# Building weighted one-hot tiles in float32 from a ring of twelve, with four PSUM banks, and moving the direct products to the node update's bank

## The reference

```
h = relu(layernorm(x))
m = relu(concat(h[src], edge_attr) @ W1 + b1) @ W2 + b2
x = x + relu(concat(h, segment_sum(m, dst)) @ U1 + c1) @ U2 + c2
h = relu(layernorm(x))
x = x + segment_sum(h[src] * edge_weight[:, None], dst)
```

## Time and profile before

| what | value |
|---|---|
| median of three runs | 2679.72 us (2676.95 to 2680.86) |
| profiled execution, its time | 2659.47 us |
| its span, first to last instruction | 2657.7 us |
| busy PE, DVE, ACT, POOL | 2049.9, 1311.2, 974.0, 1691.7 us |
| gathers issued | from 63.2 to 2203.6 us |
| first piece loaded in the second stage | 2219.6 us |
| granted TensorE clock, mean | 0.888 |

### The profile page before, as it was taken

The page is one execution under the profiler, slowest core; times in us unless marked ns, Lnnn a source line. Parts: engine busy times, 40 slices in busy tenths (PEclk is TensorE's granted clock), DMA queues, the critical chain, the costliest instruction groups (busy, mean ns, idle before and its releaser), DMA issues.

```text
span 2657.7 us, 57208 instructions
## 1 busy us (share of the span) xinstructions
PE 2049.9 (77%) x21651; PEld 1747.1 (66%) x21651; DVE 1311.2 (49%) x4334; ACT 974.0 (37%) x2419; POOL 1691.7 (64%) x1659
## 2 busy tenths in 40 slices
PE   5766666777777877777787777877778878999998
PEld 5555555656665666666666666766666767787886
DVE  6655555555555555556555555555555551111122
ACT  3334344444444444444444444444444441000111
POOL 6777777777777777777777777777777771000000
PEclk9988888888888888888888898889899899999998
DMA  3455444454444444334333333333223226999995
GB/s 88 129 169 173 162 159 159 165 171 140 142 140 148 130 132 135 118 119 127 106 109 113 99 97 94 87 94 85 74 74 82 65 62 240 401 377 384 372 350 163
DMA packets 422423, 414.27 MB, mean 156 GB/s; under 512 B 288562, under 2 KB 374178, under 8 KB 416000
## 3 DMA queue, kind: packets, MB, share of 16 engines
q1 hardware_dynamic: 369348, 354.89, 38.6%
q0 software_dynamic: 52064, 53.17, 8.8%
q10 hardware_dynamic: 732, 2.48, 0.4%
HBM read 258.64 MB, written 151.74 MB: 154 GB/s over the span
## 4 chain that ended last, share of the span: by engine, by line
POOL 62%; issue 19%; PE 9%; DMA 8%; DVE 1%; DVEq 0%; SPq 0%; ACT 0%; POOLq 0%
POOL rows L608 62%; DMA stage<-adjacency 7%; PE pair L1032 5%; PE pair L1039 1%; PE pair L1022 1%; PE pair L1045 1%; PE pair L864 1%; DMA x_all<-in_x_dram 1%; PE pair L852 0%; DVEq L1363 0%; PE pair L960 0%; PE pair L1053 0%; DVE nodes L1368 0%; DVE mean L1140 0%; SPq L490 0%
## 5 line engine op out<-in xcount | busy, mean ns | idle before, releaser
L608 POOL DMA_INDIRECT rows<-table,idx x1616 | 1649.4, 1021 | 512.0 <-issue 492.2
L721 ACT COPY stage<-pair 128x300 f32<-128x300 f32 x1616 | 622.3, 413 | 689.8 <-PE pair L946 687.3
L946 PE MATMUL pair<-bld 128*128 128x300 bf16 x4848 | 813.1, 316 | 4.5 <-DVE bld L1329 4.5
L923 PE MATMUL pair<-w1b,rings 128*128 128x128 f32 x1616 | 307.1, 349 | 530.4 <-DVE rings L1305 530.3
L923 PEld LDWEIGHTS pair<-w1b,rings 128*128 128x128 f32 x1616 | 261.2, 246 | 588.3 <-DVE rings L1305 587.9
L946 PEld LDWEIGHTS pair<-bld 128*128 128x128 bf16 x4848 | 552.2, 120 | 134.7 <-DVE bld L1329 7.9
L1329 DVE TENSOR_TENSOR bld<-bld,part 128x512 bf16<-128x512 bf16 x1212 | 432.4, 410 | 0.0
L1323 DVE TENSOR_TENSOR bld<-iota_lo,lo 128x512 bf16<-128x512 f16 x404 | 172.5, 427 | 471.1 <-PE pair L946 468.3
L1325 DVE TENSOR_SCALAR bld<-iota_key,key 128x300 bf16<-128x300 f16 x1616 | 383.5, 300 | 0.0
L1305 DVE TENSOR_TENSOR rings<-rows,pair 128x512 f32<-128x512 f32 x202 | 138.3, 685 | 461.4 <-DMA rows<-table,idx 461.4
L1032 PE MATMUL pair<-stage,h 125*64 125x96 f32 x5870 | 297.4, 253 | 25.0 <-DMA stage<-adjacency 22.2
(11 more groups left out here) (131 smaller groups left out, 779.3 us busy)
## 6 DMA issues: line engine op xcount, KB each, us to landing
stage<-adjacency SPq DMA_DIRECT2D x270, 480.0 KB, 9.4
rings<-in_edge_attr_dram SPq DMA_DIRECT2D x202, 256.0 KB
adjacency<-stage SPq DMA_DIRECT2D x28, 1200.0 KB
rows<-table,idx POOLq DMA_INDIRECT x1616
adjacency<-stage SPq DMA_DIRECT2D x20, 1080.0 KB
adjacency<-stage SPq DMA_DIRECT2D x20, 960.0 KB
adjacency<-stage SPq DMA_DIRECT2D x20, 840.0 KB
adjacency<-stage SPq DMA_DIRECT2D x20, 720.0 KB
```

The lines of the kernel that those rows point to most:

```text
L608: pool.indirect_dma_start(out=rows[:, slot, t, :], out_offset=None, in_=table, in_offset=bass.IndirectOffsetOnAxis(ap=idx[:, g, t:t + 1], ...
L721: act.copy(tiles[:, g % STAGE, :, t * WT:(t + 1) * WT], build_bank[i % 3][:, 0:KEYS].rearrange("p (h w) -> p h w", w=WT)).then_inc(tile_ke ...
L923: last = pe.matmul(bank[:, a * P:(a + 1) * P], eaT[:, slot, a, :], w1b2[:, :], start=True, stop=True)
L946: last = pe.matmul(build_bank[i % 3][:, 0:KEYS], hot_w[q % 2][k][:, :, u], hot_key[q % 2][:, u, :], start=(k == 0), stop=(k == PARTS - 1))
```

## The change

The quads go. make_tile makes the operands of one tile in float32 with two instructions: a comparison of a row of 128 numbers with `lo`, multiplied by the weight in the same instruction, and a comparison of 300 numbers with `key`. The operands lie in a ring of twelve tiles (HOTS) and VectorE is eight tiles ahead (AHEAD). build_tile issues one float32 matmul into one of four banks, instead of three bfloat16 ones into three. `key`, `lo` and the weight are kept in float32; the split of the weight ahead of the loop is gone, and so is one constant that GpSimd made. The fourth bank was `u_bank[0]` of the direct products; these now use 96 columns at the end of the second half of pair 1, whose first 375 are the node update's. Since a bank is shared, the two take turns: the node update begins at an odd step (UPDATE[c] = SUMMED[c] | 1: 23, 43, 63, 83, 103, 123, 143, 165, 185, 203), its three parts are two steps apart, and each waits until the direct product before it was copied out, as the direct products wait for the update's copies. READY[c] is UPDATE[c] + 8. The loops have three more steps at the end.

```diff
-    READY = [SUMMED[c] + 6 for c in range(CHUNKS)]
+    UPDATE = [SUMMED[c] | 1 for c in range(CHUNKS)]
+    READY = [UPDATE[c] + 8 for c in range(CHUNKS)]
...
-        build_bank = [pair[2][:, 0, :], pair[2][:, 1, :], pair[3][:, 0, :]]
+        mid_bank = pair[1][:, 1, 0:SPLIT * NP]
+        direct_bank = pair[1][:, 1, 512 - COLS:512]
+        build_bank = [pair[2][:, 0, :], pair[2][:, 1, :], pair[3][:, 0, :], pair[3][:, 1, :]]
...
             def build_tile(g, t):
                 i = g * T + t
-                q, u = i // 4, i % 4
-                if u == 0:
-                    pe.wait_ge(quad_made, q + 1)
-                wait_count(pe, tile_kept, i - 2)
-                for k in range(PARTS):
-                    last = pe.matmul(build_bank[i % 3][:, 0:KEYS], hot_w[q % 2][k][:, :, u], hot_key[q % 2][:, u, :],
-                                     start=(k == 0), stop=(k == PARTS - 1))
-                last.then_inc(tile_built, 1)
+                pe.wait_ge(tile_hot, i + 1)
+                wait_count(pe, tile_kept, i - BUILDS + 1)
+                pe.matmul(build_bank[i % BUILDS][:, 0:KEYS], hot_w[:, i % HOTS, :], hot_key[:, i % HOTS, :], start=True,
+                          stop=True).then_inc(tile_built, 1)
...
             def direct(b, half):
...
+                for c in range(CHUNKS):
+                    since = 2 * b + 2 + half - UPDATE[c]
+                    if since in (1, 3):
+                        pe.wait_ge(g_staged, 2 * c + (since + 1) // 2)
+                    if since == 5:
+                        pe.wait_ge(x1_made, c + 1)
...
             def make_g(c, half):
+                wait_count(pe, direct_kept, direct_by(UPDATE[c] + 2 * half))
...
-            dve.tensor_copy(part[0][:, :, :], wgt).then_inc(w_split, 1)
-            dve.tensor_tensor(w_left, wgt, part[0][:, :, :], ALU.subtract).then_inc(w_split, 1)
...
-            def make_quad(q):
-                g, t = q // 2, q % 2 * 4
-                wait_count(dve, tile_built, 4 * (q - 1))
-                dve.tensor_tensor(hot_eq[q % 2], iota_lo[:, :, :], over(lo[:, g, t:t + 4], P), ALU.is_equal).then_inc(eq_made, 1)
-                for u in range(4):
-                    dve.tensor_scalar(hot_key[q % 2][:, u, :], iota_key[:, :], key[:, g, t + u:t + u + 1], None,
-                                      ALU.is_equal)
-                dve.wait_ge(eq_made, q + 1)
-                for k in range(PARTS):
-                    last = dve.tensor_tensor(hot_w[q % 2][k], hot_eq[q % 2], over(part[k][:, g, t:t + 4], P), ALU.mult)
-                last.then_inc(quad_made, 1)
+            def make_tile(i):
+                g, t = i // T, i % T
+                wait_count(dve, tile_built, i - HOTS + 1)
+                dve.tensor_scalar(hot_w[:, i % HOTS, :], iota_key[:, 0:P], lo[:, g, t:t + 1], wgt[:, g, t:t + 1],
+                                  ALU.is_equal, ALU.mult)
+                dve.tensor_scalar(hot_key[:, i % HOTS, :], iota_key[:, :], key[:, g, t:t + 1], None,
+                                  ALU.is_equal).then_inc(tile_hot, 1)
```

More of the change, by code:

```diff
@@ L9 @@
 I32 = mybir.dt.int32
-BF16 = mybir.dt.bfloat16
-F16 = mybir.dt.float16
 AX_X = mybir.AxisListType.X
@@ L31 @@
 STAGE = 4
+HOTS = 12
+AHEAD = 8
 SPLIT = 3
@@ L219, in build @@
         rel = sb("rel", [P, GROUPS, T])
-        key = sb("key", [P, GROUPS, T], F16)
-        lo = sb("lo", [P, GROUPS, T], F16)
-        part = [sb(f"part{k}", [P, GROUPS, T], BF16) for k in range(PARTS)]
+        key = sb("key", [P, GROUPS, T])
+        lo = sb("lo", [P, GROUPS, T])
+        wgt = sb("wgt", [P, GROUPS, T])
         rings = sb("rings", [P, 3 * TWO * T * D + TWO * T * (D + 1)])
@@ L233, in build @@
         key_now = sb("key_now", [P, T])
[L236 to L250, removed]
+        bld = sb("bld", [P, HOTS * (P + KEYS)])
+        assert PIECES * 4 * BLK * GC <= STAGE * ROW
+        hot_w = bld[:, 0:HOTS * P].rearrange("p (s e) -> p s e", s=HOTS)
+        hot_key = bld[:, HOTS * P:].rearrange("p (s c) -> p s c", s=HOTS)
         s_back = bld[:, 0:SLOTS * COLS].rearrange("p (s c) -> p s c", s=SLOTS)
@@ L747, in fast_groups @@
                 keep_eaT(1, 1, ea_bank)
-                for s in range(GROUPS + 6):
+                for s in range(GROUPS + 9):
                     if s < GROUPS:
@@ L978, in make_up @@
                 pe.wait_ge(g_staged, 2 * c + 2)
+                wait_count(pe, direct_kept, direct_by(UPDATE[c] + 4))
                 for b in range(BLK):
@@ L1340, in fast_groups @@
             def fast_groups():
-                make_quad(0)
-                make_quad(1)
-                for s in range(GROUPS + 6):
+                for i in range(AHEAD):
+                    make_tile(i)
+                for s in range(GROUPS + 9):
                     if s < GROUPS:
@@ L1348, in fast_groups @@
                         add_sums(s - 1)
-                    for q in (2 * s + 2, 2 * s + 3):
-                        if q < 2 * GROUPS:
-                            make_quad(q)
+                    for i in range(s * T + AHEAD, (s + 1) * T + AHEAD):
+                        if i < TILES:
+                            make_tile(i)
                     for c in range(CHUNKS):
-                        if s == SUMMED[c] + 3:
+                        if s == UPDATE[c] + 5:
                             add_up(c, mid_bank[0:NP, 0:BC])
                             centre(2)(c, 0)
-                        if s == SUMMED[c] + 4:
+                        if s == UPDATE[c] + 6:
                             variance(2)(c, 0)
-                        if s == SUMMED[c] + 5:
+                        if s == UPDATE[c] + 7:
                             stage_h2(c, 0)
```

52 lines of the change are left out of this document (20 added, 32 removed).

## The result

The changed kernel takes 2786.12 us (median of 4 runs, 2776.16 to 2802.28), the kernel before, run beside it, 2680.29: a ratio of 1.0403, 95% interval 1.0352 to 1.0454. It is 4% slower; 2595 us, 3% faster, was forecast. The profiled execution took 2776.16 us.

A forecast was written before the change was run, and what follows sets the result against it. GpSimd's gathers, by number times length plus issue, were taken to bound the first stage. Terms -113.6 + 19 + 3 + 6.5 = -85 us gave 2679.7 - 85 = 2595 us, range 2566 to 2655.

The forecast's parts named there:

- The bound: First stage: time is the number of gathers times their length plus 0.305 us issue each; no gather waits for `pre_made`.
- What is removed: Gathers: lengthening beside the old VectorE instructions and weight split goes, -113.6 us; about 10.3 of 123.9 us remain.
- the gather waits for the streaming part alone and gets in between two instructions of a row: Gathers beside new VectorE instructions: held only 159 or 68 ns per instruction, as read off L1325.
- +19 us: Gathers' first need, 0.13 us in: waits for the new instructions' streaming part, 66 ns mean when held; bounds 0 and 80.
- the +3 us at the end: Gathers' end: 0.09 us can be made up, only the 159 ns instruction exceeds that; bounds 0 and 19 us.
- Rival (2): Gathers beside VectorE rows: rows without a pause shut them out until the row is over; +104 us, 2699 us; chance 0.12.
- the count of 29: Gathers that started within 50 ns ahead of three L1329 and waited for the third's end; taken as 29 of 202 rows.
- The rule that I weighed: Gathers: a VectorE instruction locks GpSimd out for its whole length; 80 instead of 19 us, 2656 us; chance 0.10.
- PE: Matmuls: 300-column records 0.25 us apart, a group costs 0.9 us more, hidden under the gathers.
- The second stage: After the gathers: later READY makes 11 pairs of batch and chunk be stored and loaded again, +6.5 us (5.6 to 7.0).
- New lengths: VectorE's new float32 comparisons: 378 ns for 300 numbers and 287 ns for 128.
- The range of the forecast: Whole kernel: 2566 to 2655 us; the forecast's own case, 2580 to 2615 us, had chance 0.60.

The follow-up runs named there:

- turns alone: The kernel before with UPDATE, READY, the waits and the direct products' bank of the changed kernel, quads and bfloat16 kept: ratio 0.9996.
- changed, another session: The changed kernel unaltered, run again beside its version with three build banks: ratio 1.0119 to the kernel before.
- three banks: The changed kernel with three build banks instead of four, nothing else: ratio 0.996 to the kernel before.
- three banks, another session: The changed kernel with three build banks instead of four, run again beside the four-bank one: ratio 1.0152 to the kernel before.
- ring of six: The changed kernel with HOTS 6 and AHEAD 4 instead of 12 and 8, four banks kept: 2654.36 us in one execution.
- pause at every tile: The changed kernel, but VectorE waits for the end of a tile's pair of comparisons before starting the next pair: 2602.69 us in one execution.
- pause at every second: The changed kernel, but VectorE waits for its own end at every second tile, making rows of four instructions: 2588.63 us in one execution.
- wide one in PSUM: The changed kernel with three build banks; only the comparison of 300 numbers reads its row from PSUM: 2580.84 us in one execution.
- weighed one in PSUM: The changed kernel with three build banks; only the weighed comparison of 128 numbers reads its row from PSUM: 2554.2 us in one execution.
- both in PSUM: The changed kernel with three build banks; both comparisons of a tile read their row of numbers from PSUM: 2549.0 us, ratio 0.9528.
- the four-bank kernel of the same session: The changed kernel unaltered, run again in a session in which engines stand still: ratio 1.0227 to the kernel before.

## Why the prediction was wrong

**The bound** was read rightly: 62 to 64% of the chain is POOL's, no gather waits. The sum over the median accounts for all that followed. Span less that sum, in the ordinary sessions (us):

| kernel | span | over the median | rest |
|---|---|---|---|
| before | 2657.7 | 123.9 | 2533.8 |
| turns alone | 2668.3 | 132.0 | 2536.3 |
| changed | 2774.3 | 239.4 | 2534.9 |
| changed, another session | 2726.2 | 189.8 | 2536.4 |
| three banks | 2653.5 | 116.6 | 2536.9 |
| three banks, another session | 2732.7 | 194.8 | 2537.9 |
| ring of six | 2652.5 | 109.0 | 2543.5 |
| pause at every tile | 2600.9 | 62.9 | 2538.0 |
| pause at every second | 2586.8 | 48.5 | 2538.3 |
| wide one in PSUM | 2579.0 | 43.0 | 2536.0 |
| weighed one in PSUM | 2552.4 | 14.0 | 2538.4 |
| both in PSUM | 2547.2 | 9.1 | 2538.1 |

The rest stays within 10 us in all of them, through 218 us more busy time of TensorE's tile matmuls (1031.4 against 813.1), other rings, banks and turns.

**What is removed** was right in kind and size: of 123.9 us some 10 were to stay, and with new instructions that read PSUM 9.1 do.

**The step that failed** is "the gather waits for the streaming part alone and gets in between two instructions of a row. I take that over". It was read off rows of four 16-bit instructions and carried to rows of sixteen float32 ones. The new rows leave less room: in the changed kernel no gather that was held for over 0.10 us got in behind an L1308, and those that got in behind an L1310 had often missed the same place before (once in the gather of 2049.39 us, five times in that of 1991.64). The count that it was read off is short too: of some 300 gathers that are 0.13 us in while an L1325 runs 68 are lengthened, 38 by an L1325 and the rest by the L1323 or L1329 that had not ended yet. In place of +19 us the new instructions cost 239.4 - 9.1 = 230 us in one profile and 181 in the other. It covers both terms, the +19 us at the start (131 measured) and the +3 us at the end (106), which rested on a VectorE instruction that could be held off for 0.09 us; the gathers were held off instead. Rival (2), at 0.12, came nearest: rows shut gathers out for more than 3 us. But it had them all wait to the row's end, which 36 of the 122 long ones do, took over the count of 29 where 124 are over 0.56 us longer, and did not have the shut-outs at the end at all; its 104 us stand against some 180 to 230. The step is shown false by the pause, which brings back most of the loss with every instruction unchanged. With rows out of the way the single instructions cost 34 and 5 us, 39 together beside the forecast's 19 for both, and not in its order: most of it was to be the wide one's.

The rule that I weighed, that the lock lasts for the whole instruction (the Trainium skill's page "SBUF — State Buffer", section "SBUF: two separate sides"), gave 80 us. The traces agree with its distance at the end of a gather (0.13 us measured, about 0.115 stated) and with its warning, but not with the size: a lock for the length of one instruction alone makes no wait of 3.2 us beside instructions of 0.37, as at 1991.64 us. The page says nothing of rows.

**PE** was right: the changed kernel's two records of a tile are 0.253 us apart in the median at full clock, and PE still waits for the sums that VectorE makes of the gathered rows, and not the gathers for PE:

```profile
DVE rings L1290 <- DMA rows<-table,idx: 1065.2, 200, 9.5
...
PE pair L913 <- DVE rings L1290: 474.3, 162, 7.1
```

**The second stage** was to grow by 6.5 us. To be read beside the earlier trace rows:

```profile
2334.80 1.40 SPq L482 DMA_DIRECT2D stage<-adjacency  x3
```

```profile
2334.80:2774.30 439.50, 401.56 (x6620) 344.62 (x6620) 71.49 (x321) 47.62 (x207) 0.00 (x0) 0.98 0.96 350
```

The stage takes 439.5 us against 438.1; 441.8 and 442.4 with the turns alone and with both comparisons in PSUM. So it grew by 1.4 to 4.3 us, and the ratio of 0.9996 for the turns alone has room for either. **New lengths**: 0.38 and 0.29 us were forecast, 0.381 and 0.351 measured; the second scalar operand costs 0.06 (0.298 without it against 0.357 in the four-bank kernel of the same session).

**The spread** was missed altogether. The kernel before repeats within 0.5% of its median in a session, and its median within 0.4% between the ordinary ones; the changed kernel is at 1.012 and 1.040, and its three-bank version at 0.996 and 1.015. Two profiles of the changed kernel have the sums 239.4 and 189.8, two of the three-bank one 116.6 and 194.8. Where the gathers fall in the rows does differ: in the profile with 116.6, 95 of them are 0.13 us in when the seventh instruction of a row runs and 23 are held for over 0.56 us, in the other 50 and 101. What shifts them was not found. The range of the forecast came from one profile and allowed for nothing of the kind.

**Open** is why a row closes, and what opens it again behind its eighth or twelfth instruction. It needs instructions with a tensor input in SBUF, it does not need the second scalar, rows of two and of four behind a wait do not close, and rows of sixteen do, though not for every gather that meets one. The ring of six has mostly rows of fourteen and sixteen too and its longest gather is 3.94 us, so it tells nothing here. Whether the streamed length (some 0.16 of the 0.29 us from start to start, by the forecast's rate) or the number in a row decides was tried only in a session in which engines stand still.

## What to carry to other kernels

Where GpSimd's indirect DMAs set the time, cost every VectorE instruction beside them by how it reads SBUF, not by its length: a pair that reads PSUM takes 0.18 us longer (516 + 398 against 381 + 351 ns) and made the kernel 4 to 8% faster than the same pair reading SBUF (0.953 against 0.996 to 1.040). Long unbroken rows of such instructions are the worst; a wait for VectorE's own end at every second tile, which costs VectorE time, was worth 3 to 7% (2588.63 / 2671.97 = 0.969 in one execution, against the same 0.996 to 1.040). What a short row shows does not hold for a long one: when a forecast hangs on that, it is the first thing to try alone. And one session does not give such a kernel's time: run it in several, each beside the kernel before.

## What the runs showed of the hardware

A gather has two needs that VectorE can keep from it: one 0.13 us into it, after which it ends 0.8 us behind the instruction that held it, with two tensor inputs or with one of float32, and one at its end, after which it ends 0.10 to 0.15 us behind. In rows of sixteen float32 comparisons that read SBUF the first was kept from a gather for up to 3.2 us (4139 against 944 ns), the second for up to 3.4 us (4336 ns). With a wait of VectorE for its own end behind every pair the first was kept for 0.44 us at most, and the second in 4 gathers, for 0.1 us together. With the row of numbers of all three comparisons in PSUM, all gathers past the first 100 us lay between 0.938 and 0.961 us. A gather held for more than 0.10 us was let in behind the wide comparison of a pair, never behind the weighed one, in the changed kernel. And in two sessions the same kernel took 3370 instead of 2675 us, with ScalarE standing still for up to 33.2 us at a time; what held it, and whether it goes with the chip, was not found.
